# Unread products only where the planned busy share of TensorE is under 0.8

## The reference

```
layer 0:  x = attn(ln(x)) + x                 # 16 heads of 16, q, k, v rounded to 8 bits, and softmax rounded to 8 bits
          x = attn(ln(x), context) + x        # the same, keys and values from a second input
          x = a * gelu(g) @ ff_w2 + x         # (a, g) = split(ln(x) @ ff_w1), 1024 wide
layer 1:  x = layernorm(x + attn(x, x, x, causal))          # float32, nothing rounded
          x = layernorm(x + attn(x, context, context))
          x = layernorm(x + moe(x))           # 8 experts, the best 2 of each token, 256 -> 1024 -> 256
```

## Time and profile before

| | us |
|---|---|
| time, median of 3 runs | 3578.2 |
| lowest and highest | 3574.54, 3578.53 |
| the profiled execution, its own time | 3593.65 |
| its span, first to last instruction | 3591.9 |
| transformer part, to the last TensorE product of it | about 2689 |
| experts part | the rest, some 900 |
| mean granted clock of TensorE | 0.919 |

### The profile page before, as it was taken

The page is one execution under the profiler, slowest core; times in us unless marked ns, Lnnn a source line. Parts: engine busy times, 40 slices in busy tenths (PEclk is TensorE's granted clock), DMA queues, the critical chain, the costliest instruction groups (busy, mean ns, idle before and its releaser), DMA issues. The chain is left out here.

```text
span 3591.9 us, 54697 instructions
## 1 busy us (share of the span) xinstructions
PE 3051.4 (85%) x18207; PEld 1719.0 (48%) x18207; DVE 2111.3 (59%) x4295; ACT 1893.7 (53%) x3859; POOL 1593.6 (44%) x2792
## 2 busy tenths in 40 slices
PE   6888999898899989899998989888885399999960
PEld 3435444443544454354444435443425177777850
DVE  4877887786788778678877867854352000000016
ACT  4665767567576766757675675735341032223210
POOL 5655554582565467257546725642301500000026
PEclk9999999999999999999999999988985599999985
DMA  3005221541422143042204313132303345455523
GB/s 86 16 27 109 57 65 30 115 95 30 99 61 54 30 92 71 28 83 58 56 28 92 70 29 84 40 75 54 55 9 116 134 147 170 159 171 172 175 73 114
DMA packets 270054, 290.11 MB, mean 81 GB/s; under 512 B 32056, under 2 KB 255680, under 8 KB 269808
## 3 DMA queue, kind: packets, MB, share of 16 engines
q1 hardware_dynamic: 261936, 270.21, 30.0%
q0 software_dynamic: 6144, 16.79, 1.4%
q10 hardware_dynamic: 1728, 0.01, 0.0%
HBM read 224.34 MB, written 62.39 MB: 80 GB/s over the span
## 5 line engine op out<-in xcount | busy, mean ns | idle before, releaser
L1250 ACT ACTIVATE probs<-ps,nbias,sc 128x512 f32<-128x512 f32 x1024 | 790.4, 778 | 275.5 <-DVE nbias L1131 216.9
L997 POOL TENSOR_SCALAR pq<-probs,rstep 128x512 f16<-128x512 f32 x1024 | 709.7, 693 | 252.0 <-PE ps L1364 168.4
L1148 DVE TENSOR_REDUCE m<-ps 128x1 f32<-128x512 f32 (+3 forms) x1024 | 561.1, 583 | 294.0 <-PE ps L1390 150.8
L1128 DVE TENSOR_REDUCE nmax<-ps 128x2 f32<-128x1024 f32 x512 | 620.8, 1212 | 95.4 <-PE ps L1356 94.8
L1387 PE MATMUL ps<-kst,qst 96*128 96x512 bf16 (+3 forms) x1024 | 331.4, 355 | 90.5 <-issue 50.7
L1140 DVE TENSOR_SCALAR big<-ps 128x1024 bf16<-128x1024 f16 x512 | 348.1, 680 | 63.1 <-PE ps L1364 61.4
L1364 PE MATMUL ps<-id,pq 128*128 128x128 f16 x4096 | 330.5, 226 | 47.5 <-DVE big L1140 41.3
L1875 DVE COPY yb<-moe_ps 128x256 f32<-128x256 f32 x78 | 33.1, 425 | 569.5 <-PE moe_ps L1725 569.5
L1409 PE MATMUL ps<-qst,kst 108*128 108x512 bf16 (+3 forms) x1024 | 306.3, 353 | 65.2 <-ACT big L1269 29.9
L1629 POOL DMA_INDIRECT got<-rows_out,slot_of x64 | 69.5, 1085 | 643.1 <-DMA rows_out<-yb 624.5
L1364 PEld LDWEIGHTS ps<-id,pq 128*128 128x128 f16 x4096 | 261.5, 101 | 192.1 <-issue 129.3
(11 more groups left out here) (205 smaller groups left out, 4621.7 us busy)
## 6 DMA issues: line engine op xcount, KB each, us to landing
e_w<-in_L_xattn_e_w_dram SPq DMA_DIRECT2D x78, 1024.0 KB
wring<-in_L_xattn_ff_w_dram SPq DMA_DIRECT2D x96, 256.0 KB, 2.9
parts<-parts_sb SPq DMA_DIRECT2D x64, 384.0 KB, 3.0
kst<-parts SPq DMA_DIRECT2D x192, 128.0 KB, 4.8
qst<-parts SPq DMA_DIRECT2D x192, 128.0 KB, 5.1
moe_in<-rows_in SPq DMA_DIRECT2D x39, 256.0 KB
rows_out<-yb SPq DMA_DIRECT2D x39, 256.0 KB, 2.2
rows_in<-zero SPq DMA_DIRECT2D x19, 512.0 KB, 4.0
```

The source lines that it names most:

```text
L997: nc.gpsimd.tensor_scalar(pq[:, u % 2, h, :], probs[:, u % 2, h, :], rstep[:, u % 2, h:h + 1], HALF_ROUND, ALU.mult, ALU.add).then_inc(SIG ...
L1128: nc.vector.tensor_reduce(nmax[:, n % 2, :], ps[:, a:a + 2, :], AX.X, ALU.max, negate=True).then_inc(SIG["M"], 1)
L1148: nc.vector.tensor_reduce(m32[:, g % 2, t, h:h + 1], bank(("A", B, s, n))[:, 0:width], AX.X, ALU.max, negate=True).then_inc(SIG["am"], 1)
L1250: nc.scalar.activation(probs[:, u % 2, h, :], ps[:, BANKS[("S", B, s, u)][h], :], ACT.Exp, bias=nbias[:, u % 2, h:h + 1], scale=sc[:, s:s ...
```

## The change

The planner now remembers TensorE's planned busy intervals, unread products among them, and adds a condition to the loop that puts in unread products: it goes on only while the planned busy share of TensorE in the 3.4 us before `free["PE"]` is under 0.8. The condition is asked before each `W`, so the loop ends at the first point at which the share is 0.8 or more, and nothing more is put into that gap.

```diff
@@ constants @@
 WARM_GAP = 0.4
+WINDOW = 3.4
+WARM_SHARE = 0.8
 AHEAD = 0.05
@@ program_order @@
     order = []
 
+    used = collections.deque()
+
+    def busy_before(now):
+
+        while used and used[0][1] <= now - WINDOW:
+            used.popleft()
+        return sum(b - max(a, now - WINDOW) for a, b in used) / WINDOW
+
...
-        while engine == "PE" and t - free["PE"] >= WARM_GAP:
+        while engine == "PE" and t - free["PE"] >= WARM_GAP and busy_before(free["PE"]) < WARM_SHARE:
             idle = [bank for bank in held if (bank == 7 or not exact_open) and
                     (held[bank] is None or ended.get(drain_of(*held[bank]), 1e9) <= free["PE"])]
             if not idle:
...
             order.append(extra)
+            used.append((free["PE"], free["PE"] + TAKES["W"]))
             free["PE"] += TAKES["W"]
...
         free[engine] = t + takes(*e)
+        if engine == "PE":
+            used.append((t, free[engine]))
         ended[e] = free[engine] + (LANDS[kind] if kind in LANDS else TAIL[engine])
```

## The result

| us | before | after |
|---|---|---|
| median of 15 runs each, side by side | 3578.53 | 3589.11 |
| lowest and highest | 3574.11, 3587.82 | 3583.66, 3593.72 |
| ratio after to before | | 1.0026, 95% interval 1.0018 to 1.0034 |
| profiled execution, its own time | 3593.65 | 3593.72 |
| its span | 3591.9 | 3592.0 |

The changed kernel is slower by 0.26%, 9.3 us by the ratio and 10.6 by the medians. The forecast was 3583.0 with a range of 3573 to 3594, "slower in sign and probably within 0.2%": the sign came out, the size was twice the +4.8 that was forecast. It is more than the 0.2% within which it was expected to stay; of the forecast's own range, +1 to +10, the ratio's 9.3 lies inside and the medians' 10.6 just outside.

The account below looks back on a forecast made before the run. TensorE, 85% busy, was taken as the bound, with chains of single steps at head and tail. Empty gaps +6.8 and removed products -2.0 gave +4.8 on the median 3578.2: 3583.0 us, range 3573 to 3594.

Parts of the forecast that it names:

- the first rival: Batches 1 to 6: clock falls once per batch, +12, 3595 us, or twice, +24, 3607 us; chance 0.13.
- gap at 130: Gap left idle 5.5 us; eight transposes and q behind it run partly at half clock: +1.5 us.
- gap at 224.5: Gap left idle 3.9 us; half clock behind it delays the gate projections leading to gelu and layer 1: +2.0 us.
- gap at 2578.4: Gap left idle 5.6 us; transposes, kept products and first half of q slow down: +1.1 us.
- gap at 2682.9: Gap left idle 2.5 us; last projection at half speed for 3.0 to 5.9 us: +2.2 us, least certain.
- Which products go: 360 of 737 unread products stay; 97, 173 and 107 go in head, steady part and tail.
- pack of 10 at 52.3: All 10 unread products at 52.3 us go, and the next scores come earlier: -0.25 us.
- products in the way of T: Transposes at 2362.26 us stood behind 11 unread products; four stay, so they start earlier: -1.4 us.
- gap at 2591.1: 37 of 42 unread products go; VectorE's maxima set the pace there at either clock: 0.
- The head: First transposes start 4.8 us earlier behind 13 instead of 38 products, hidden by the load issued at 41.27: 0.
- In batches 1 to 6 packs of 1 to 8 go: Steady batches lose short packs, most of one or two products; the forecast's sum has no loss for them.
- Thinned stretches fall too: The first rival: thinned steady batches let the clock fall, 2.0 us per fall, 3595 or 3607 us; chance 0.13.

Follow-up runs that it names:

- long gaps only: Kernel before, with the busy-share condition asked only in planned gaps of 2.5 us or more: 3594.79 us, ratio 1.0008.
- short gaps only: Kernel before, with the busy-share condition asked only in planned gaps under 2.5 us: 3600.25 us, ratio 1.0029.
- asked again: Changed kernel, but at a share of 0.8 or more the loop steps on 0.1 us and asks again; against the kernel before 3594.58 us, ratio 1.0003.
- the first experiment: Same run as long gaps only: kernel before, condition only in planned gaps of 2.5 us or more; 3594.79 us, ratio 1.0008.
- the sixth experiment: Kernel before, with the second sequence's load moved right behind the first eight weight pieces: 3585.43 us, ratio 0.9979.
- second experiment: Same run as short gaps only: kernel before, condition only in planned gaps under 2.5 us; 3600.25 us, ratio 1.0029.
- ninth: Kernel before, with the busy-share condition asked only in planned gaps under 1.0 us: 3597.11 us, ratio 1.0015.
- tenth: Kernel before, with the busy-share condition asked only in planned gaps from 1.0 to 2.5 us: 3598.74 us, ratio 1.0017.

## Why the prediction was half right

The time lies in the range of 3573 to 3594, but the sum did not bring it there: it had half of the loss, and the room above it was left for the first rival.

Block by block, the length of the same stretch of real products in the traces, us. In the experiments whose edit does not touch a block, it differs from before's by at most 0.6, 0.1, 0.1, 0.5, 0.8 and 1.1 us, from the first row to the last:

| stretch | before | after | long gaps only | short gaps only | asked again |
|---|---|---|---|---|---|
| first scores to 121 us | 71.34 | 73.15 | 72.83 | 71.30 | 71.31 |
| around the gap at 130 | 17.53 | 20.43 | 19.07 | 18.69 | 17.52 |
| around the gap at 224.5 | 15.84 | 18.35 | 16.95 | 15.79 | 15.79 |
| up to T of batch 7 | 29.48 | 27.69 | 28.17 | 29.90 | 29.30 |
| around the gap at 2578.4 | 18.65 | 20.32 | 20.78 | 18.76 | 20.14 |
| last stretch, with the gap at 2682.9 | 49.38 | 50.65 | 48.79 | 48.54 | 49.24 |

**Which products go.** Forecast 360 left, found 358; in the three stretches 97, 173 and 107 gone, found 98, 172 and 109 (the one at 219.6 stands in two answers). Right.

**The long gaps, term by term.** The delay of the first product behind each place less that of the last one ahead of it, us:

| place | forecast | after | long gaps only |
|---|---|---|---|
| pack of 10 at 52.3 | -0.25 | +1.8 | +1.5 |
| gap at 130, to behind q | +1.5 | +1.5 | +1.9 |
| gap at 224.5, to the gate | +2.0 | +2.1 | +1.1 |
| products in the way of T | -1.4 | -1.9 | -1.4 |
| gap at 2578.4, to second half of q | +1.1 | +1.0 | +2.3 |
| gap at 2591.1, to the scores | 0 | +1.2 | +0.3 |
| gap at 2682.9, the last projection | +2.2 | +1.7 | 0.0 |

The clock fell behind all four of the forecast's gaps in the changed kernel, and these four terms held: +6.8 forecast, +6.3 found. With the long gaps alone they give +5.3, with no fall behind the last one, so that the last term came true in the changed kernel is partly luck. The first row of the table did not hold: the forecast saw the scores come 0.25 earlier without the pack, and did not ask what the clock would do there. It stayed at 0.50 for 8 us longer, and the products that follow came 1.8 us later. By the runs, the long gaps were forecast at +4.8 and measured at +2.9 (-1.4 to +7.2) in the first experiment.

**The head.** The pack shrank and the transposes start 3.5 us earlier (I had -4.8), the scores 0.4 us earlier. Forecast 0, and right in its reason, as the sixth experiment shows. In order of time, the load, the statistics that waited for it and the scores of the changed kernel, which answer to the earlier trace rows:

```profile
24.86 1.09 PE L1308 MATMUL ps<-id,xn 128*128 128x128 f32 x8 [0.51 <-POOL xn L980]
...
41.06 1.06 SPq L858 DMA_DIRECT2D X<-in_x_dram  x2
...
45.10 0.75 DVE L1072 BATCH_NORM_STATS2 bn<-X 128x6 f32<-128x256 f32 x2 [24.07 <-DMA X<-in_x_dram]
...
49.51 0.61 PE L1369 MATMUL ps<-kmask,qi 32*128 32x512 bf16 x4 [10.80 <-DVE qi L1103]
```

The idle time before the scores grew from 6.12 to 10.80: the gain is there, as waiting.

**The step that failed.** "In batches 1 to 6 packs of 1 to 8 go" was costed at nothing, and so were the short gaps of the head and the tail. The forecast read one stall, in which the clock was 1.00 over the first 2.5 us of idling, and took from it that holes of 2 us are safe; the same trace had the falls at 1971.5 to 1992.0 us, with no wait over 1.05 us ahead of them. The clock fell behind the holes of 1.5 to 1.8 us at 120.7, 438.2 and 755.5 all the same, and in the head, where untouched blocks agree to 0.1 us, that at 120.7 added 1.4 us and the one at 215.8 another 0.8. What differs in the traces is the work ahead: before the stall TensorE was busy for 4.40 of 4.40 us, before the hole at 438.2 for 3.80 of 4.20 and before that at 120.7 for 4.02 of 4.70. That this is the reason is argued only, and the last gap, where the same idling with nearly the same work ahead ended both ways, says that it is not all of it. The rival "Thinned stretches fall too" came about in its mechanism, one to two falls per batch; its price per fall, 2.0, was too high: the six new falls of the changed kernel cost 1.1, 1.5, 1.5 and three times nothing. By the runs the short gaps cost 10 us (second experiment) where the sum had 0, and the steady part has 4.7 of them, give or take as much (-0.4 to +9.3). This is the term that was mis-sized most; the 2.0 us at the pack of 10 and the 1.2 at the gap at 2591.1 come behind it.

The Trainium skill, page "TensorE: Matmul & The Clock Gate", Part 1, "HAM oscillation", prices a fall at the throttled time times one half. Every half-clock record of the transformer added up gives 287 us before and 341 after; by the page the 55 us more would cost an estimated 27. The two traces show +15.3 and the runs +9.3, so here the rule is an upper end. Of the 55, 26 lie in the first 255 us, 17 of them in the one fall at 44.1 (7 before), which began in the wait for the first scores. The same page's "A second HAM failure mode: psum-queue depth-cycling" says that frequent micro-idles between groups of products are enough to make the clock swing. The prediction did not weigh it, and the ninth and tenth experiments agree with it.

**What stays open.** Why the gaps under 1 us are worth 0.15%: the ninth experiment's trace shows one fall per batch, but only its first four are its own, so which gap lets each fall happen was not settled. How much of the steady part's loss is the edit's: kernels with nothing edited there differ by up to 10 us over it. And the experts' front, which took 73.7 us in the one profile of the changed kernel and 83.7 to 88.8 in all others.

## What to carry to other kernels

An unread product is worth what the clock behind it is worth. The first products of a gap behind dense work could be left out at no measurable cost, the whole gap could not: a rule that stops at the first sign of enough should ask again before the gap ends. The length of a gap does not tell whether it is safe: three in five of the products taken out (240 against 158, by the second and the first experiment) stood in planned gaps under 2.5 us, and there, by the two ratios, the larger part of the loss was (their intervals overlap). And a filler must never wait for what the next real product waits for; where it can start only when that one could, it is pure delay.

## What the runs showed of the hardware that was not expected

The clock fell behind idle stretches of 1.5 to 1.8 us, and then for 3.4 us, where the stall of the earlier trace rows, over 9 us long, had shown 1.00 over its first 2.5; in the kernel before it fell with no wait over 1.05 us ahead of it (1981.8 us, 4.84 of the 6.70 us before it busy). The fall can come after the idling: in the changed kernel at 2697.0 the clock was 1.00 over the whole 2.5 us of idling and 0.51 over the 3.5 us of dense work that followed. And it can stay away after the same idling: 2.57 us ahead of the last projection ended in 0.51 in the changed kernel and in 1.00 in the first experiment. Whole busy shares hide it: 3.66 of 4 us busy at 0.59, and 3.71 of 4 at 1.00, are the same 4 us of the clock in two kernels.
